# VectorE adds the fifth early group, ScalarE's queue issues half of the late loads, and the last group is normalised in two halves

## The reference

```python
x = _layernorm(x + attention(x))              # 8 heads, relative bias
x = _layernorm(x + mlstm(x, ctx, ctx))        # 4 heads, gated
x = _layernorm(x + ffn(x))
# ffn: shared expert + the two most probable of 8 experts per token, + x
probs = softmax(x @ router_w); top_k_prob, top_k_idx = top_k(probs, 2)
out = expert(x, shared) + sum(top_k_prob * expert(x, routed[top_k_idx])) + x
# _layernorm: (x - mean) / sqrt(var + 1e-5), over the 128 numbers of a token
```

## Time and profile before

| What | Value |
|---|---|
| median of 3 runs | 449.33 us |
| lowest and highest | 447.81 and 451.22 us |
| the profiled execution's own time | 447.76 us |
| its span, first to last instruction | 445.7 us |
| TensorE matmul busy | 421.6 us (95%) |
| VectorE busy | 317.2 us (71%) |
| ScalarE busy | 298.1 us (67%) |
| GpSimd busy | 190.2 us (43%) |

### The profile page before, as it was taken

How to read it: one execution, slowest core, us unless ns; L and a number is a source line. 1 busy time by engine, 2 the same in 40 slices (tenths; PEclk the granted TensorE clock), 3 DMA queues, 4 the chain that set the end, 5 groups by cost and what they waited for, 6 DMA issues and landing times.

```text
span 445.7 us, 14337 instructions
## 1 busy us (share of the span) xinstructions
PE 421.6 (95%) x5098; PEld 365.9 (82%) x5099; DVE 317.2 (71%) x999; ACT 298.1 (67%) x649; POOL 190.2 (43%) x220
## 2 busy tenths in 40 slices
PE   7999999989998899999988999989998999999994
PEld 6688888878887776776665898989998999999963
DVE  5568888888888878989897668885444445443964
ACT  4678778768767498987965976336665665336654
POOL 5620220220810012221858665645777766554430
PEclk9999999999999999999999999999999999999999
DMA  4343242850000005311212225221232432326436
GB/s 139 88 132 83 57 109 57 178 163 1 4 2 26 2 26 177 101 40 46 69 62 67 62 73 131 74 55 41 76 91 79 107 90 80 84 74 200 168 120 189
DMA packets 47630, 38.11 MB, mean 86 GB/s; under 512 B 5088, under 2 KB 40928, under 8 KB 47568
## 3 DMA queue, kind: packets, MB, share of 16 engines
q1 hardware_dynamic: 42816, 28.16, 23.5%
q0 software_dynamic: 4320, 8.92, 5.9%
q10 hardware_dynamic: 432, 0.20, 0.2%
HBM read 19.30 MB, written 16.34 MB: 80 GB/s over the span
## 4 chain that ended last, share of the span: by engine, by line
PE 52%; DVE 26%; ACT 9%; issue 7%; DMA 3%; POOL 2%; DVEq 1%; SPq 0%; ACTq 0%; POOLq 0%
PE bank L1503 7%; PE bank L1471 5%; PE bank L1461 5%; PE bank L1416 4%; DVE tkr L1636 2%; DVE negmax L1645 2%; DVE prob L1642 2%; PE bank L1077 2%; PE bank L1130 2%; PE bank L1120 2%; PE bank L1079 2%; DMA routed<-rh,zbuf 2%; PE bank L1078 2%; PE bank L1490 2%; PE bank L1492 2%
## 5 line engine op out<-in xcount | busy, mean ns | idle before, releaser
L661 POOL DMA_INDIRECT routed<-rh,zbuf x71 | 70.5, 993 | 45.6 <-DVE rh L2060 29.8
L2060 DVE TENSOR_SCALAR rh<-bank,zbuf 128x128 f32<-128x128 f32 x71 | 24.8, 349 | 44.1 <-PE bank L1503 21.9
L1503 PE MATMUL bank<-wdn,prob 128*128 x384 | 47.3, 275 | 1.3 <-DVE rh L2060 1.3
L1503 PEld LDWEIGHTS bank<-wdn,prob 128*128 128x128 f32 x384 | 45.2, 192 | 1.7 <-DVE rh L2060 1.7
L557 POOL DMA_INDIRECT slots<-zbuf,slot x32 | 33.3, 1041 | 18.1 <-issue 5.8
L994 ACT ACTIVATE prob<-bank 128x512 f32<-128x512 f32 x48 | 28.6, 597 | 16.2 <-PE bank L1492 13.5
L557 POOL DMA_INDIRECT slots<-tkr,slot x32 | 32.1, 1004 | 13.1 <-issue 5.5
L694 ACT ACTIVATE prob<-prob 128x512 f32<-128x512 f32 x32 | 20.2, 630 | 15.9 <-DVE prob L1646 15.8
L1490 PE MATMUL bank<-xT_hi,wq_hi 128*128 128x256 f32 x96 | 29.0, 302 | 1.3 <-DVE xT_lo L2070 1.3
L1416 PEld LDWEIGHTS bank<-sdn,qblk 128*128 128x128 f32 x256 | 29.7, 192 | 0.5
L1416 PE MATMUL bank<-sdn,qblk 128*128 128x128 f32 x256 | 29.9, 275 | 0.0
(11 more groups left out here) (338 smaller groups left out, 1206.1 us busy)
## 6 DMA issues: line engine op xcount, KB each, us to landing
slots<-x2T SPq DMA_DIRECT2D x8, 585.0 KB, 5.2
zbuf<-slots SPq DMA_DIRECT2D x24, 130.0 KB, 2.5
tkr<-in_x SPq DMA_DIRECT2D x8, 256.0 KB, 3.1
cs<-in_ctx SPq DMA_DIRECT2D x8, 256.0 KB, 2.9
wup<-in_L_ffn_routed_up SPq DMA_DIRECT2D x1, 2048.0 KB, 8.6
zbuf<-tkr SPq DMA_DIRECT2D x8, 256.0 KB, 2.7
out_x<-x2T SPq DMA_DIRECT2D x8, 256.0 KB
tkr<-routed SPq DMA_DIRECT2D x6, 256.0 KB, 3.3
```

The lines of the kernel that those rows point to most:

```text
L661: pool.indirect_dma_start(routed, bass.IndirectOffsetOnAxis(ap=xr[n][:, :].bitcast(I32)[:, DEST:DEST + 1], axis=0), yr[n % 4][:, :], None) ...
L1503: m = mm(bank[6 + a][:, 0:D], hTp[:, q, c // 2, c % 2, a, :], wdn[:, bass.ds(e * (FC * D) + c * D, D)], start=(c == 0), stop=(c == FC - 1))
```

## The change

The routed rows of group 4 (the fifth early group) are added by VectorE and no longer by TensorE: its two `early_add` stand between the row products of the last two tiles, its totals and moments behind the tiles of groups 2 and 3. TensorE's `early_sums` is left with group 5, in bank 2. The late loads of `y1` are issued by ScalarE's queue, behind its tiles of group 1; SyncE issues those of `y0` and stores group 0 after them. The moments, aggregates and roots of group 7 are done for its first two tiles and then for its last two, with VectorE's tiles of group 6 between. ScalarE has two tiles of group 6 where it had four, VectorE the other two. The shift is formed for the first two tiles of group 7 alone, which are ScalarE's.

```diff
-BY_DVE_SUMS = EG - 2
+BY_DVE_SUMS = EG - 1
...
-    FIN = {t: (2 + (t // GT) % 2, t % GT) for t in range(BY_DVE_SUMS * GT, EARLY)}
+    FIN = {t: (2, t % GT) for t in range(BY_DVE_SUMS * GT, EARLY)}
...
-    A_TILES = [4, 4, 0, 0, 4, 0, 4, 2]
+    A_TILES = [4, 4, 0, 0, 4, 0, 2, 2]
+
+    def expert_rows(k, g):
+        return routed[k * B * S:(k + 1) * B * S, :].rearrange("(p t) d -> p t d", t=NT)[:, g * GT:g * GT + GT, :]
...
-        for g in (2, 0):
-            result_out(g)
+        result_out(2)
         for n in range(4):
             sp.wait_ge(sc_y[n], 16 * len(range(n, SLOT_TILES, 4)))
         for g in range(EG, NG):
-            sums_in(g, y0, y1)
-        for g in (3, 1, 5, 4, 6, 7):
+            sp.dma_start(y0[:, g * GT:g * GT + GT, :], expert_rows(0, g)).then_inc(ld_y[g - EG], 16)
+        for g in (0, 3, 1, 5, 4, 6, 7):
             result_out(g)
...
-        last_rstd(1, EG - 2, EG)
-        last_act(EG - 2, 2)
-        last_rstd(2, EG, EG + 1)
-        last_act(EG, 3)
-        last_rstd(3, EG + 1, NG)
-        last_act(NG - 1, 4)
+        for n in range(4):
+            act.wait_ge(sc_y[n], 16 * len(range(n, SLOT_TILES, 4)))
+        for g in range(EG, NG):
+            act.dma_start(y1[:, g * GT:g * GT + GT, :], expert_rows(1, g)).then_inc(ld_y[g - EG], 16)
+        last_rstd(1, (EG - 2) * GT, EARLY)
+        group_act(EG - 2, 2)
+        last_rstd(2, EARLY, EARLY + GT)
+        group_act(EG, 3)
+        last_rstd(3, EARLY + GT, EARLY + GT + 2)
+        last_rstd(4, EARLY + GT + 2, NT)
+        group_act(NG - 1, 4)
...
+        in_loop = 2 * BY_DVE_SUMS - 2
...
         y_out(SLOT_TILES - 2, SLOT_TILES - 2, (SLOT_TILES - 2) // 4)
+        early_add(in_loop)
+        early_add(in_loop + 1)
         y_out(SLOT_TILES - 1, SLOT_TILES - 1, (SLOT_TILES - 1) // 4)
...
-        shifts(0, 0, EG - 2)
+        shifts(0, 0, (EG - 2) * GT)
         rest(2)
         rest(3)
-        statistics(EG - 2)
-        statistics(EG - 1)
-        shifts(1, EG - 2, EG)
+        for q in range(in_loop, 2 * BY_DVE_SUMS):
+            early_total(q)
+        for q in range(in_loop, 2 * BY_DVE_SUMS):
+            early_stats(q)
+            early_mean(q)
+        statistics(0, BY_DVE_SUMS * GT, EARLY, 1)
+        shifts(1, (EG - 2) * GT, EARLY)
         rest(EG - 1)
-        statistics(EG)
-        shifts(2, EG, EG + 1)
-        statistics(NG - 1)
-        shifts(3, EG + 1, NG)
+        statistics(1, EARLY, EARLY + GT, 3)
+        shifts(2, EARLY, EARLY + GT)
+        statistics(2, EARLY + GT, EARLY + GT + 2, 4)
+        rest(EG)
+        statistics(3, EARLY + GT + 2, NT, 5)
+        shifts(3, EARLY + GT, EARLY + GT + 2)
+        dve.wait_ge(s["rstd2_ok"], 5)
         rest(NG - 1)
```

More of the change, by code:

```diff
@@ L427, in sums_in @@
             for k, y in enumerate((first, second)):
[L428 to L429 removed]
+                sp.dma_start(y[:, r, :], expert_rows(k, g)).then_inc(ld_y[g], 16)
         def result_out(g):
@@ L1022, in last_rstd @@
         def last_rstd(n, lo, hi):
-            r = slice(lo * GT, hi * GT)
-            act.wait_ge(s["mv2_ok"], GT * hi)
+            r = slice(lo, hi)
+            act.wait_ge(s["mv2_ok"], hi)
             act.activation(lnf[:, r], mvf[:, r, 1], ACT.Ln, bias=eps[:, 0:1]).then_inc(s["lnv_ok"], 1)
@@ L1027, in last_rstd, with group_act @@
             act.activation(rstdf[:, r], lnf[:, r], ACT.Exp, scale=-0.5).then_inc(s["rstd2_ok"], 1)
-        def last_act(g, shifts):
+        def group_act(g, shifts):
             act.wait_ge(s["shift_ok"], shifts)
@@ L1033, in last_act @@
             m.then_inc(s["fina_ok"], 1)
-        last_rstd(0, 0, EG - 2)
-        last_act(0, 1)
-        last_act(1, 1)
-        last_rstd(1, EG - 2, EG)
-        last_act(EG - 2, 2)
-        last_rstd(2, EG, EG + 1)
-        last_act(EG, 3)
-        last_rstd(3, EG + 1, NG)
-        last_act(NG - 1, 4)
+        last_rstd(0, 0, (EG - 2) * GT)
+        group_act(0, 1)
+        group_act(1, 1)
+        for n in range(4):
[9 more added lines that the diff above has]
+        group_act(NG - 1, 4)
     @block.tensor
@@ L1531, in sums @@
             r, to = late_part(q)
-            pe.wait_ge(ld_y[q // 2], 64)
+            pe.wait_ge(ld_y[q // 2], 32 + 32)
             mm(to, ident[:, :], y0[:, r, :], start=False, stop=False, skip_group_check=True)
@@ L2108, in early_total @@
         def early_total(q):
-            dve.wait_ge(s["early_ok"], 2 * q + 1)
+            dve.wait_ge(s["early_ok"], 2 * q + 1 if q < in_loop else in_loop + q + 1)
             r = slice(2 * q, 2 * q + 2)
@@ L2113, in early_stats @@
         def early_stats(q):
-            dve.wait_ge(s["early_ok"], 2 * q + 2)
+            dve.wait_ge(s["early_ok"], 2 * q + 2 if q < in_loop else in_loop + q + 3)
             if q >= 2:
@@ L2124, in early_mean @@
                 dve.bn_aggr(mvf[:, 2 * q + k, :], stats[:, 2 * (q % 2) + k, :]).then_inc(s["mv2_ok"], 1)
-        first_sum = SLOT_TILES - 2 * BY_DVE_SUMS
+        first_sum = SLOT_TILES - in_loop
         for t in range(first + 2, SLOT_TILES):
@@ L2130, in _, with statistics @@
             q = t - first_sum
-            if 0 <= q < 2 * BY_DVE_SUMS:
+            if 0 <= q < in_loop:
                 early_add(q)
-            if 0 <= q - 1 < 2 * BY_DVE_SUMS:
+            if 0 <= q - 1 < in_loop:
                 early_mean(q - 1)
             y_out(t - 2, t - 2, (t - 2) // 4)
-            if 0 <= q < 2 * BY_DVE_SUMS:
+            if 0 <= q < in_loop:
                 early_total(q)
                 early_stats(q)
-        early_mean(2 * BY_DVE_SUMS - 1)
+        early_mean(in_loop - 1)
         y_out(SLOT_TILES - 2, SLOT_TILES - 2, (SLOT_TILES - 2) // 4)
+        early_add(in_loop)
+        early_add(in_loop + 1)
         y_out(SLOT_TILES - 1, SLOT_TILES - 1, (SLOT_TILES - 1) // 4)
-        def statistics(g):
-            dve.wait_ge(s["tot_ps"], g - BY_DVE_SUMS + 1 if g < EG else 2 + 2 * (g - EG) + 2)
-            dve.wait_ge(s["mv2_ok"], GT * g)
-            for k in range(GT):
-                m = dve.bn_stats(stats[:, k, :], total(g * GT + k))
+        def statistics(n, lo, hi, sums):
+            dve.wait_ge(s["tot_ps"], sums)
+            dve.wait_ge(s["mv2_ok"], lo - lo % GT)
+            for t in range(lo, hi):
+                m = dve.bn_stats(stats[:, t % GT, :], total(t))
             m.then_inc(s["stat_ok"], 1)
-            pause(dve, s["stat_ok"], NT + BY_DVE_SUMS + g + 1, s["passed_dve"])
-            for k in range(GT):
-                dve.bn_aggr(mvf[:, g * GT + k, :], stats[:, k, :]).then_inc(s["mv2_ok"], 1)
+            pause(dve, s["stat_ok"], NT + 2 * BY_DVE_SUMS + n + 1, s["passed_dve"])
+            for t in range(lo, hi):
+                dve.bn_aggr(mvf[:, t, :], stats[:, t % GT, :]).then_inc(s["mv2_ok"], 1)
         def shifts(n, lo, hi):
-            r = slice(lo * GT, hi * GT)
+            r = slice(lo, hi)
             dve.wait_ge(s["rstd2_ok"], n + 1)
```

2 lines of the change are left out of this document (removed).

## The result

In the first timing the changed kernel takes 449.31 us in the median of 12 runs (447.8 to 451.82), and the kernel before, in 12 runs of its own, 446.4 us, not the 449.33 of the three runs that were shown. The ratio is 1.0049, 95% interval 1.0026 to 1.0072: the change costs 1.2 to 3.2 us. Two more timings on other occasions gave 1.0053 (1.0023 to 1.0084) and 1.0015 (0.9993 to 1.0038). So it is slower, by some 0.4% on average, though the third interval by itself leaves room for no change. That is under the 1% that was called measurable; the intervals reach 0.2 to 0.3% to each side. All ratios and averages are over the fast runs, those at most 1.5% above the kernel's fastest.

A forecast was written before the change was run, and what follows sets the result against it. No single engine was taken to hold the end; group 6 was bound by TensorE's queue, by 0.46 us, its load right behind. Terms -0.46 - 0.36 + 0.64 = -0.2 took 449.33 to 449.1 us; range 447.3 to 451.0.

The forecast's parts named there:

- the landing of group 6's loads: Late loads before group 6's sums: landing 3.2 us after the issue at 431.62, so at 434.8 instead of 435.2.
- The removed sums: TensorE's queue before group 6: one early group less frees 2.58 us, of which only 0.46 us comes through.
- The issue on ScalarE's queue: Group 6's second load, issued beside the first at 431.62 instead of 432.00: 0.36 us gained after the hand-over.
- the first rival: Group 6's landing doesn't move, both queues sharing sixteen DMA engines: +0.2, or +0.9 with a 4.3 us landing; chance 0.25.
- The halves: Group 6's moments to the last tile, with group 7 in halves: 5.91 us instead of 5.27, so 0.64 us longer.
- VectorE's extra work: Group 4's adds, moments and aggregates on VectorE lie wholly in its former waits and cost nothing.
- the last scatter: Scatter of the last expert rows keeps its time; a rival had it up to 0.5 us later, chance 0.03.
- Group 7 in time: Group 7's loads, last issued 1.3 us earlier, are in time if landed by 437.9; rival of late landing, chance 0.05.
- TensorE's clock: Rival: after a 1.7 us hole before group 6's sums, half clock makes the end 2 us later; chance 0.02.

## Why the prediction was wrong

The median lay inside the range, but only because that range was laid around three runs of before whose median was 2.9 us over that of twelve. The forecast itself, 0.2 us faster, is refuted: the change is slower. The step that failed most is the landing of group 6's loads. By the prediction's sum the first sum of group 6 starts 3.22 us after the first issue, 0.8 us sooner than before (-0.46 and -0.36). In the five profiles of the changed kernel it starts after 4.26 on average, 0.2 later than before, so this step is 1.0 us off. The clock adds 0.3 on average, 0.7 in two profiles of five. The halves came out 0.2 cheaper than forecast, and the way to the first issue 0.1 shorter. Point by point:

- **The removed sums, -0.46.** Right that TensorE's queue ends 2.5 us sooner (fillers end 1.6 us after the first issue, before 4.1) and that only the way to the landing could come through. Wrong that 0.46 would: this took the one old landing of 3.2 us from its issue as the rule, and it is the shortest of the seven on record in one queue. Where TensorE waited for the load in one queue, the first sum came 3.90, 4.00, 4.02, 4.24, 4.71, 5.01 and 5.75 us after the first issue. The old 4.04 is near the best that this route gives.
- **The issue on ScalarE's queue, -0.36.** The issue moved as foretold (430.16 beside 430.14) and the landing did not follow: first sums at 4.53, 4.08, 4.17, 4.11 and 4.39 us. I took 3.2 us from issue to landing "because the nearest row is this very load"; on ScalarE's queue it is 4.0 to 4.5. This is the first rival, with chance 0.25, and its mechanism too: SyncE's load beside it takes 3.6 us where it took 3.0. The Trainium skill's "DMA: Bandwidth & Descriptors", section "Issuing engines are not separate DMA queues", says that issuing from several engines saves only the time to initiate; the traces agree, and of the 0.38 us that the issue came sooner nothing is seen in the landing. Whether the second queue is slower in itself stays open, since no run has a load on it alone. Its first sums lie between the best and the worst of the single queue's, but the worst three are those with a held-up issue; without them the single queue gives 3.90 to 4.24.
- **The halves, +0.64.** Right in kind and sign; measured +0.45 against the old profile, 0.54 against a whole last group whose sums are in time. The 0.2 us too much was in the hand-overs, which overlap: VectorE starts its second moments at 440.92 before its tiles' 0.70 us from 440.31 are over, and ScalarE's tiles start at 442.27, ahead of the root's end.
- **VectorE's extra work, 0, and the last scatter, 0.** Right. Product to first issue is 4.18 to 4.34 us in all 18 profiles: 4.18 to 4.25 in the eight that store group 0 behind the late loads, 4.28 to 4.34 in the ten that store it ahead. Groups 4 and 5 are normalised by 434.4, 3 us before group 6's moments.
- **Group 7 in time.** Right: in all five profiles of the changed kernel its moments start 2.09 or 2.10 us after group 6's. GpSimd's scatter and group 0's store behind the loads cost nothing visible.
- **TensorE's clock, chance 0.02.** Wrong twice. The hole was put at 1.7 us and was 2.46 to 2.92, because the loads landed later than forecast; in all nine profiles with 1.86 us or less the clock did stay at 1.00. And I argued from the earlier trace rows that TensorE, without work since 439.9, kept 1.00 until 444.0, and so would keep it through a shorter hole. But a hole that runs at 1.00 doesn't vouch for what follows: in the first profile after, the hole stands at 1.00, and 0.50 comes 1.13 us behind the first sum. TensorE lost the clock after 2.4 to 3.2 us without work in four of seven profiles, and in both with more. It costs 0.7 us in the changed kernel and up to 1.8 in the variants, less than the 2 us of the rival; in the changed kernel part of the sums runs before the clock falls.

At full clock the changed tail is 16.1 us against 15.66, +0.4 to +0.5; at half clock 17.0 to 17.2. With two of five at half the mean is 16.5, +0.9 us or 0.2%. The timings say 0.49, 0.53 and 0.15%, and the first two have lower ends at 0.26 and 0.23%. So the halves are shown, by adding them alone and by taking them away, and the clock in the tail by the profiles in which TensorE had work nearly until the load landed; that they are the whole of the measured loss is not. What stays open is about 1 us on average: upstream half clock was no less frequent in some kernels with full clock in the tail, and before itself has only one profile here, whose landing was a good one, the shortest in one queue. In three of the nine profiles with one queue a held-up issue made the first sum 0.7 us or more later, and before can meet that too.

## What to carry to other kernels

Work taken off an engine is worth only the way to the next thing that is late; if that is a DMA, look at how its landing spreads over several profiles before its one value is put into a sum. A second queue of issues made one load start sooner and its neighbour land later: price the pair, not the one. Taking work from TensorE can cost more than it gives where the hole that it leaves ends in matmuls on the critical path: keep it filled until the data lands (20 fillers instead of 8 did that here), and count the hole (2.4 to 6.2 us where it went wrong here) as a risk, not as time saved. Splitting the last group into halves cost 0.54 us here, since VectorE, which both halves need, also had two tiles to normalise in between; that it would pay with another engine in between is not shown.
